# Attention and mixture of experts on one core: products with the values as one block per step, maxima turned as one square

## What is computed

```python
xt = jnp.transpose(x, (0, 2, 1))
q = xt @ Wq.T                                  # heads of dk = 16
scores = scale * jnp.einsum('bhqd,bhkd->bhqk', qh, qh)
logits = (scores * cmask + (1.0 - cmask) * NEG) * rmask
attn = jax.nn.softmax(logits, axis=-1)
ctx = jnp.einsum('bhqk,bhkd->bhqd', attn, qh)
out = ctx @ Wo.T                               # then transposed back
```

## The kernel before

| | TensorE | ScalarE | VectorE |
|---|---|---|---|
| 0 | | copy_hidden | |
| 1 | apply_probs, second half | copy_products | find_top |
| 2 | turn_max, project_q | copy_q | copy_max |
| 3 | turn_products | write_max | normalize |
| 4 | turn_values | | find_best, mark_best |
| 5 | turn_context | exp_gap, copy_v | |
| 6 | apply_probs, first half | copy_context | |
| 7 | project_out | | make_gate |

## Time and profile before

### The profile page before, as it was taken

How to read it: one execution, slowest core, us unless ns; L and a number is a source line. 1 busy time by engine, 2 the same in 40 slices (tenths; PEclk the granted TensorE clock), 3 DMA queues, 4 the chain that set the end, 5 groups by cost and what they waited for, 6 DMA issues and landing times.

```text
span 252.9 us, 5416 instructions
## 1 busy us (share of the span) xinstructions
PE 226.8 (90%) x1713; PEld 145.7 (58%) x1713; DVE 147.4 (58%) x403; ACT 132.9 (53%) x321; POOL 112.1 (44%) x206
## 2 busy tenths in 40 slices
PE   7988899989999999999999998499983799999970
PEld 5987556665666576657666554256541455555630
DVE  3786857868886888788878666436311122232320
ACT  2431577758767777777778887234311233333310
POOL 4755646624652464346001130631676146575351
PEclk9999999999999999999999999959999689999996
DMA  5685756997759766575533100460355024433100
GB/s 167 180 194 135 189 159 198 264 224 219 204 147 267 207 171 180 144 214 161 141 106 111 50 26 23 110 188 21 92 179 139 34 84 115 113 105 101 60 18 0
DMA packets 44731, 34.39 MB, mean 136 GB/s; under 512 B 5708, under 2 KB 42719, under 8 KB 44704
## 3 DMA queue, kind: packets, MB, share of 16 engines
q1 hardware_dynamic: 26896, 18.77, 27.3%
q0 software_dynamic: 2944, 8.24, 11.5%
q10 hardware_dynamic: 14864, 7.04, 11.1%
HBM read 16.91 MB, written 7.28 MB: 96 GB/s over the span
## 4 chain that ended last, share of the span: by engine, by line
PE 71%; DMA 8%; ACT 4%; DVE 3%; SPq 3%; issue 3%; ACTq 1%; another core or an unknown queue 1%; POOL 1%; POOLq 0%; DVEq 0%
PE bank L704 13%; PE bank L585 11%; PE bank L561 10%; PE bank L573 9%; PE bank L724 6%; PE bank L722 4%; PE bank L695 3%; DMA stack<-max_rows 3%; PE bank L614 3%; PE bank L526 3%; SPq L426 3%; ACT probs L785 3%; PE bank L606 2%; DMA stack<-parts 2%; PE bank L595 2%
## 5 line engine op out<-in xcount | busy, mean ns | idle before, releaser
L918 DVE TENSOR_REDUCE row_max<-bank 128x2 f32<-128x512 f32 x128 | 84.8, 687 | 24.1 <-PE bank L561 23.9
L785 ACT ACTIVATE probs<-bank 128x512 f32<-128x512 f32 x128 | 76.2, 600 | 25.2 <-PE bank L573 22.6
L561 PE MATMUL bank<-stack 96*128 96x256 bf16 x256 | 49.5, 274 | 1.7 <-DMA stack<-parts 1.5
L573 PE MATMUL bank<-stack 99*128 99x256 bf16 x256 | 49.0, 273 | 1.8 <-DMA stack<-max_rows 1.1
L386 POOL DMA_INDIRECT out<-y_sb,put_i x23 | 23.1, 1006 | 33.3 <-DVE y_sb L1184 28.0
L704 PE MATMUL bank<-gu_sb,gotT 128*128 x92 | 34.9, 506 | 0.0
L585 PE MATMUL bank<-probs,v_sb 128*32 128x256 f32 x512 | 34.3, 385 | 0.2 <-ACT probs L785 0.2
L561 PEld LDWEIGHTS bank<-stack 96*128 96x128 bf16 x256 | 21.2, 98 | 19.4 <-DVE row_max L918 10.4
L294 POOL TENSOR_TENSOR qm<-q_sb,cond_all 128x256 f32<-128x256 f32 x15 | 10.9, 729 | 45.4 <-ACT q_sb L770 45.4
L1176 DVE SCALAR_TENSOR_TENSOR act_sb<-silu,got,bank 128x176 f32<-128x176 f32 x23 | 9.1, 397 | 37.0 <-ACT silu L866 26.4
L376 POOL DMA_INDIRECT got<-rows_dram,take_i x23 | 22.5, 979 | 18.2 <-DVE take_i L1073 9.4
(11 more groups left out here) (154 smaller groups left out, 295.8 us busy)
## 6 DMA issues: line engine op xcount, KB each, us to landing
stack<-parts SPq DMA_DIRECT2D x96, 64.0 KB, 2.6
stack<-parts ACTq DMA_DIRECT2D x96, 64.0 KB, 2.7
gu_sb<-in_guT SPq DMA_DIRECT2D x8, 352.0 KB, 3.9
rows_dram<-h_sb SPq DMA_DIRECT2D x16, 132.5 KB, 2.4
x_sb<-in_x SPq DMA_DIRECT2D x16, 128.0 KB, 3.7
rows_dram<-in_x SPq DMA_DIRECT2D x4, 512.0 KB, 5.1
cond_all<-in_cond SPq DMA_DIRECT2D x12, 128.0 KB, 4.2
dn_sb<-in_dnT SPq DMA_DIRECT2D x4, 256.0 KB, 4.0
```

Source lines behind the costliest of these rows:

```text
L561: mm = t_.matmul(bank[h % 2][:, q * T:(q + 1) * T], stack[k][0:ROWS, 0, h, q * P:(q + 1) * P], stack[k][0:ROWS, 1, h, :], start=True, stop ...
L573: mm = t_.matmul(bank[2 + h % 2][:, q * T:(q + 1) * T], stack[k][0:ROWS2, 0, h, q * P:(q + 1) * P], stack[k][0:ROWS2, 1, h, :], start=True ...
L785: a.activation(probs[:, h, :, :].rearrange("p k t -> p (k t)"), bank[2 + h % 2][:, 0:NT * T], ACT.Exp, scale=float(DK) ** -0.5).then_inc(e ...
L918: v.tensor_reduce(row_max[:, b % 2, :, h:h + 1], bank[h % 2][:, 0:NT * T].rearrange("p (q k) -> p q k", q=NT), AX.X, ALU.max).then_inc(max ...
```

## The change

The products of a batch become one block of 32 matmuls in slot 2 of step s = b+3 (batch 15 keeps its old slots 6 and 1). `probs` gets a second home, and the exponentials wait for the products two batches back. The post work moves back: copy_products from slot 1 to 3, turn_products 3 to 4, normalize 3 to 4, turn_context 5 to 6, copy_context 6 to 7, project_out from slot 7 to slot 0 of the next step up to step 16, copy_hidden from 0 to 1, the router's choice to slot 2. turn_values goes from 4 to 5, copy_v from 5 to 6, project_q from 2 to 1. For the last batch most of the work stays where it was (`post`). The maxima are kept by head and half; both bfloat16 parts (2 x 16 columns) stand in one 128 x 128 tile whose other columns are zero, and TensorE turns that as one transpose. Then 32 rows of 128 values go to the stack, where there were 16 of 256.

```diff
+    NM = NH * NT
...
-        row_max = sb("row_max", [P, 2, NT, NH])
-        max_parts = sb("max_parts", [P, 2, NT, 2, NH], BF16)
-        max_rows = sb("max_rows", [2 * NH, 2, T], BF16)
-        probs = sb("probs", [P, NH, NT, T])
+        row_max = sb("row_max", [P, 2, NH, NT])
+        max_parts = sb("max_parts", [P, 2, P], BF16)
+        max_rows = sb("max_rows", [2 * NM, 2, P], BF16)
+        probs = sb("probs", [P, 2, NH, NT, T])
...
+        def post(s, slot):
+            return slot - 1 if s - 3 == B - 1 else slot
...
+            g.memset(max_parts[:, :, 2 * NM:P], 0.0).then_inc(consts_made, 1)
@@ split_max @@
-                g.tensor_copy(max_parts[:, k, :, 0, :], row_max[:, k, :, :]).then_inc(max_hi_made, 1)
+                maxima = row_max[:, k, :, :].rearrange("p h q -> p (h q)")
+                g.tensor_copy(max_parts[:, k, 0:NM], maxima).then_inc(max_hi_made, 1)
@@ turn_max @@
-                to = bank[VM][:, :].bitcast(BF16)
-                for q in range(NT):
-                    mm = t_.transpose(to[0:2 * NH, q * P:(q + 1) * P],
-                                      max_parts[:, b % 2, q, :, :].rearrange("p a h -> p (a h)"), ident_b[:, :])
-                mm.then_inc(max_turned, 1)
+                t_.transpose(bank[VM][:, :].bitcast(BF16)[:, 0:P], max_parts[:, b % 2, :], ident_b[:, :]).then_inc(max_turned, 1)
@@ TensorE, after both scores of slot h @@
-                    if h == 1 and there(s - 3):
+                    if h == 0 and there(s - 4) and s <= B:
+                        project_out(s - 4)
+                    if h == 1 and there(s + 3):
+                        project_q(s + 3)
+                    if h == 1 and s - 3 == B - 1:
                         apply_probs(s - 3, 1)
                     if h == 2:
                         if there(s - 1):
                             turn_max(s - 1)
-                        if there(s + 3):
-                            project_q(s + 3)
+                        if there(s - 3) and s - 3 < B - 1:
+                            apply_probs(s - 3, 0)
+                            apply_probs(s - 3, 1)
                         if s == B + 2:
                             table_early()
-                    if h == 3 and s == B:
+                    if h == post(s, 4) and there(s - 3):
+                        turn_products(s - 3)
+                    if h == 4 and s == B:
                         rank_early()
-                    if h == 3 and there(s - 3):
-                        turn_products(s - 3)
-                    if h == 4 and there(s):
+                    if h == 5 and there(s):
                         turn_values(s)
-                    if h == 6 and there(s - 2):
+                    if h == 6 and s - 2 == B - 1:
                         apply_probs(s - 2, 0)
-                    if h == 5 and there(s - 3):
+                    if h == post(s, 6) and there(s - 3):
                         turn_context(s - 3)
-                    if h == 7 and there(s - 3):
+                    if h == 7 and there(s - 3) and s >= B:
                         project_out(s - 3)
@@ exponential @@
-                if h % HG == 0 and b > 0:
-                    act.wait_ge(pv_done, NG * (b - 1) + h // HG + 1)
+                if h % HG == 0 and b > 1:
+                    act.wait_ge(pv_done, NG * (b - 2) + h // HG + 1)
@@ ScalarE, after the exponential and the DMA issue of slot h @@
-                    if h == 0 and there(s - 4):
+                    if h == (1 if s <= B else 0) and there(s - 4):
                         copy_hidden(s - 4)
-                    if h == 1 and there(s - 3):
-                        copy_products(s - 3)
                     if h == 2 and there(s + 3):
                         copy_q(s + 3)
+                    if h == (1 if s - 3 == B - 1 else 3) and there(s - 3):
+                        copy_products(s - 3)
                     if h == 3 and there(s - 1):
                         write_max(s - 1)
...
-                    if h == 5 and there(s):
+                    if h == 6 and there(s):
                         copy_v(s)
-                    if h == 6 and there(s - 3):
+                    if h == post(s, 7) and there(s - 3):
                         copy_context(s - 3)
@@ VectorE, after the reduction of slot h @@
-                    if h == 1 and there(s - 4):
+                    if h == (2 if s <= B else 1) and there(s - 4):
                         find_top(s - 4)
...
+                    if h == 2 and there(s - 4) and s < B:
+                        find_best(s - 4)
+                        mark_best(s - 4)
...
-                    if h == 3 and there(s - 3):
+                    if h == post(s, 5) - 1 and s - 3 == B - 1 or h == 4 and there(s - 3) and s - 3 < B - 1:
                         normalize(s - 3)
-                    if h == 4 and there(s - 4) and s < B:
-                        find_best(s - 4)
-                        mark_best(s - 4)
-                    if h == 4 and s == B:
+                    if h == 5 and s == B:
                         early_counts()
                         early_places()
```

More of the change, by code:

```diff
@@ L312, in split_max @@
                     pool.wait_ge(max_turned, b - 1)
-                g.tensor_copy(max_parts[:, k, :, 0, :], row_max[:, k, :, :]).then_inc(max_hi_made, 1)
+                maxima = row_max[:, k, :, :].rearrange("p h q -> p (h q)")
+                g.tensor_copy(max_parts[:, k, 0:NM], maxima).then_inc(max_hi_made, 1)
                 pool.wait_ge(max_hi_made, b + 1)
-                g.tensor_tensor(max_parts[:, k, :, 1, :], row_max[:, k, :, :], max_parts[:, k, :, 0, :],
+                g.tensor_tensor(max_parts[:, k, NM:2 * NM], maxima, max_parts[:, k, 0:NM],
                                 ALU.subtract).then_inc(max_lo_made, 1)
@@ L349, in _ @@
                     g.memset(ones_b[:, :], 1.0).then_inc(consts_made, 1)
-                    pool.wait_ge(consts_made, 5)
+                    pool.wait_ge(consts_made, 6)
                     g.affine_select(out=before[:, :], in_=before[:, :], compare_op=ALU.is_gt, fill=0.0, base=0,
@@ L546, in turn_max @@
                 if b == 0:
-                    pe.wait_ge(consts_made, 3)
-                to = bank[VM][:, :].bitcast(BF16)
-                for q in range(NT):
-                    mm = t_.transpose(to[0:2 * NH, q * P:(q + 1) * P],
-                                      max_parts[:, b % 2, q, :, :].rearrange("p a h -> p (a h)"), ident_b[:, :])
-                mm.then_inc(max_turned, 1)
+                    pe.wait_ge(consts_made, 4)
+                t_.transpose(bank[VM][:, :].bitcast(BF16)[:, 0:P], max_parts[:, b % 2, :], ident_b[:, :]).then_inc(max_turned, 1)
             def scores_for_max(b, h):
@@ L585, in apply_probs @@
                         mm = t_.matmul(bank[PV][c * VC:(c + 1) * VC, g * T:(g + 1) * T], v_sb[:, b % NV, k, HG * g + c, :],
-                                       probs[:, HG * g + c, k, :], start=(k == 0), stop=(k == NT - 1))
+                                       probs[:, b % 2, HG * g + c, k, :], start=(k == 0), stop=(k == NT - 1))
                 mm.then_inc(pv_done, 1)
@@ L624, in rank_early @@
                 pe.wait_ge(added, NE)
-                pe.wait_ge(consts_made, 6)
+                pe.wait_ge(consts_made, 7)
                 pe.wait_ge(max_done, NH * B)
@@ L782, in exponential @@
                 act.wait_ge(s2_done, NH * b + h + 1)
-                if h % HG == 0 and b > 0:
-                    act.wait_ge(pv_done, NG * (b - 1) + h // HG + 1)
-                a.activation(probs[:, h, :, :].rearrange("p k t -> p (k t)"), bank[2 + h % 2][:, 0:NT * T], ACT.Exp,
+                if h % HG == 0 and b > 1:
+                    act.wait_ge(pv_done, NG * (b - 2) + h // HG + 1)
+                a.activation(probs[:, b % 2, h, :, :].rearrange("p k t -> p (k t)"), bank[2 + h % 2][:, 0:NT * T], ACT.Exp,
                              scale=float(DK) ** -0.5).then_inc(exp_done, 1)
@@ L812, in write_max @@
                 act.wait_ge(max_copied, b + 1)
-                act.dma_start(stack[b % NSTACK][ROW_MAX:ROW_MAX + 2, 1, :, :], max_rows[:, k, :]).then_inc(max_in[k], 16)
+                act.dma_start(stack[b % NSTACK][ROW_MAX:ROW_MAX + 2, 1, :, :].rearrange("a h (q t) -> a (h q) t", q=NT),
+                              max_rows[:, k, :]).then_inc(max_in[k], 16)
             act.dma_start(wq_sb[:, :], wqT).then_inc(wq_in, 16)
@@ L917, in reduce_max @@
                     dve.wait_ge(max_lo_made, b - 1)
-                v.tensor_reduce(row_max[:, b % 2, :, h:h + 1],
+                v.tensor_reduce(row_max[:, b % 2, h, :],
                                 bank[h % 2][:, 0:NT * T].rearrange("p (q k) -> p q k", q=NT), AX.X, ALU.max).then_inc(max_done, 1)
@@ L924, in copy_max @@
                     dve.wait_ge(max_in[b % 2], 16 * (b // 2))
-                v.tensor_copy(max_rows[:, b % 2, :], bank[VM][:, :].bitcast(BF16)[0:2 * NH, 0:T]).then_inc(max_copied, 1)
```

(1 more changed line is left out.)

## The result

The changed kernel takes 275.25 us (median of 4 runs, 271.98 to 281.33) against 255.92 (4 runs, 254.92 to 257.26): ratio 1.071, 95% interval 1.060 to 1.082. The forecast was 269.5 in a range of 259.5 to 277, slower with 0.88. The profiled execution took 274.69 us with a span of 272.7, and it is compared here with the 252.9 of before.

What follows compares the result with a forecast made beforehand. The prediction took TensorE to bound the attention stage, with no slack. Its terms summed to +14.0 us on the profiled 254.78, giving 268.8, taken as 269.5 because the median is 1.0 higher; range 259.5 to 277.

Steps and rivals of the forecast that it cites:

- TensorE as the bound of the step: Attention stage: every piece of the 8.39 us step is a TensorE piece, with no slack.
- The block: Products on TensorE: one block of 32 takes 1.96 us instead of 2.20 for two of 16, 0.24 saved.
- The saving at the maxima: Turned maxima and the projection behind them on TensorE: 0.34 us saved per step, bounds 0.10 to 0.34.
- The two waits: TensorE waits 1.00 us for the products' copy and 0.53 for the context's copy; step 9.40 instead of 8.39.
- before step 3: Start of attention: batch 0's two half blocks of products move behind slot 2 of step 3, -2.0 us.
- steps 3 to 13: Middle of attention: 85.58 us becomes 94.0 at 9.40 a step, +8.4 us.
- steps 13 to 16: Later attention steps, with less work in each: 23.21 us becomes 26.4, +3.2 us.
- step 16 to the last half block: End of attention, one scores pair a slot: two steps of 8.1, 11.85 us becomes 16.2, +4.4 us.
- expert stage: The stage after attention: untouched by the change, 0 us.
- The late maxima: Rival: 256-byte pieces make every landing of the maxima's DMA take 4.92 us, 0.96 more a step, 281 us; chance 0.08.
- Only the first wait binds: Rival: the projection's weights find the context's copy in time, so only the products' copy holds TensorE; 259 to 260; chance 0.10.
- faster: Rival: the waits don't bind and TensorE runs its own 7.58 us, VectorE 7.9 a step; 247.7 us; chance 0.08.

Runs made afterwards that it cites:

- run 3: Changed kernel with the square undone (two transposes of 16 columns, 16 rows of 512 bytes in the maxima's DMA): 272.37 us.
- run 11: Changed kernel with maxima's DMA, products' copy and context's copy sooner, and the maxima turned as before (two transposes): 248.2 us, ratio 0.970 to the kernel before.
- run 4: Kernel before with only the maxima turned as one square, nothing moved: 251.19 us, ratio 0.998 to the kernel before.
- run 1: Changed kernel with ScalarE copying the products at the end of slot 2 instead of behind the exponential of slot 3: 268.76 us.
- run 2: Changed kernel with ScalarE copying the context in slot 6, behind the values, instead of behind the exponential of slot 7: 262.16 us.
- run 6: Changed kernel with both copies sooner (products at the end of slot 2, context in slot 6), maxima's DMA still in slot 3: 259.96 us.
- run 7: Changed kernel with maxima's DMA, then products' copy, at the end of slot 2, and context's copy in slot 6 ahead of the values: 246.68 us, ratio 0.966 to before.
- run 5: Changed kernel with the maxima's DMA issued at the end of slot 2, both copies left in place: 276.26 us.
- run 8: Kernel before with the square, and the maxima's DMA issued at the end of slot 2 instead of slot 3: 249.22 us, ratio 0.976.
- run 10: Kernel before with the square and the maxima's DMA in slot 2, once more: 250.3 us, ratio 0.978 to the kernel before.
- run 9: Changed kernel with maxima's DMA, products' copy and context's copy sooner, once more: 249.5 us, ratio 0.976 to the kernel before.

## Why the prediction was right, and what it mis-sized

**What bounds, and what the change saves.** TensorE as the bound of the step was right; with the waits removed the step follows TensorE's pieces again. The block was right to the hundredth (1.96: measured 1.86 and 0.10). The saving at the maxima was right as a sum and given to the wrong edit: turn and projection went from 0.84 to 0.06 + 0.43, 0.35 less (forecast 0.34), but the square has only some 0.02 to 0.06 of that, as whole steps with and without it differ (runs 3 and 11). By the rows the rest comes of moving `project_q` to slot 1, out from behind the turn (0.63 became 0.43), and of the turn standing right ahead of the block: two turns cost 0.15 there and 0.21 in the old order. No run moves `project_q` alone. The square is worth its 0.29 only in the old order (run 4).

**The two waits.** Right in place and nearly in size; the second shows in eight of ten steps, since in two the maxima's landing came later still. From the start of slot 2 (103.30 in the timeline of TensorE): products copied from 3.77 (forecast 3.69), L598 at 4.40 (4.33), L617 at 8.04 (7.96), next slot 2 at 9.46 (9.40). One detail was wrong: the exponential of slot 7 is held not by its scores but by the copy of the values ahead of it on ScalarE (109.56, 110.14, 110.42 in the chain above), which comes to the same time. Runs 1, 2, 6 and 7 show both waits: take away the one or the other and the step is 8.9, take away both and it is 8.6, take away the landing as well and it is 7.90.

**The sum, term by term** (from the chains before and after):

| term | forecast | measured |
|---|---|---|
| before step 3 | -2.0 | 33.91 - 35.88 = -2.0 |
| steps 3 to 13 | +8.4 | 98.02 - 85.58 = +12.4 |
| steps 13 to 16 | +3.2 | 26.53 - 23.21 = +3.3 |
| step 16 to the last half block | +4.4 | 18.64 - 11.85 = +6.8 |
| expert stage | 0 | 95.6 - 96.4 = -0.8 |
| sum | +14.0 | 272.7 - 252.9 = +19.8 |

(Slot 2 starts with its first scores in the chain: 33.91, 131.93 and 158.46, the last being the second half of a group of four; the blocks of 32 stand at 34.63, 132.42 and 158.73.) Two terms carry the 5.8 that was missing, with 4.0 and 2.4. In steps 3 to 13 four steps are 9.78, 11.54, 10.21 and 9.96 from block to block, 3.65 us above the 9.46 of the others. The longest of them in the timeline of TensorE:

```profile
81.20 0.39 PE L576 MATMUL bank<-stack 99*128 99x256 bf16 x2 [1.58 <-DMA stack<-max_rows]
...
82.32 1.01 PE L533 MATMUL bank<-x_sb,wq_sb 128*128 128x256 f32 x2
83.13 0.63 PE L564 MATMUL bank<-stack 96*128 96x256 bf16 x2
...
84.22 2.67 PE L588 MATMUL bank<-probs,v_sb 128*32 128x256 f32 x32
86.83 0.39 PE L564 MATMUL bank<-stack 96*128 96x256 bf16 x2
```

A wait for the maxima of 1.58, and then, in the chain, L533 at 0.85 instead of 0.43 and a block of 2.60 instead of 1.86: the granted clock is 0.50 from 82.5 to 85.5 us, the lower of the two levels (1.2 instead of 2.4 GHz), and was 1.00 throughout this stage before. Set against a step of 9.46, the landings account for 1.7 of the 3.65 us (1.2 in the step of 11.54, 0.5 in that of 9.96), the lower clock for 1.6 (in the steps of 11.54 and 10.21), and the 0.3 of the step of 9.78 goes through a DMA issue of ScalarE. So only two of the four have a landing in them, not three as I had put it ahead of run 5. The prediction had the smaller margin of the maxima (3.5 us), called it hidden up to 0.5, and put nothing into the sum for it. It had no term for the clock at all. Near the end it is the same: the step that begins at 167.47 has a block of 3.34 and lasts 9.63; in run 5 that step is at full clock and lasts 8.00, what the prediction worked out as 8.1. So 1.6 of the missing 2.4 there is clock. Of the other 0.8, some 0.5 is a wait that the working passed over: from slot 2 of step 16 to that of step 17 it is 8.62, and the scores at 167.08 had waited 0.47 for an exponential of ScalarE. The rest I haven't traced.

That 275.3 lies inside the range of 259.5 to 277 is thus in part luck. The range had room for some tenths a step for late DMAs, but the 3.2 us of lower clock had no term and no bound.

**The late maxima.** Nothing points to the 256-byte pieces as their cause. The same DMA in pieces of 512 bytes made TensorE wait six times in run 3, with landings of 3.9 to 4.8 us in its chain against 3.8 to 5.3 in the changed kernel. By the Trainium skill (DMA: Bandwidth & Descriptors, Specifications) transfers under 512 bytes are read, modified and written; no run here shows a cost of it. What counts is when the DMA is issued: from slot 2 there is no wait for it in the new order (runs 5 and 7), and one of 0.2 us in the old (run 8). The rival that every landing is late (0.08, 281) is refuted too: in the kernel after two steps of ten were longer for it.

**The chances.** "Only the first wait binds" and "faster" got 0.18 together and both were refuted by the list of waits. "Faster", that nothing holds TensorE, needed three instructions of ScalarE in other slots; then its number (7.9 us a step, 247.7 us) is what was measured (7.90, 246.7 and 249.5).

## What to carry to other kernels

When a step is moved back by a slot on every engine, its consumer may come to stand closer behind its producer than the latency between them: place the step again, engine by engine, with the measured start-to-start times, and ask of each copy what it is queued behind. A copy that depends only on the long block belongs right behind the block, where its engine is idle anyway (ScalarE for 1.41 us here), not behind the next head's work. And two savings at the same change from wide to narrow columns don't add up (0.29 in the old order, 0.02 to 0.06 beside the block).

## What the hardware showed that I had not expected

- The clock of TensorE fell to half (0.50 granted, for 3 to 7 us) inside the attention stage in six of the twelve profiled executions of other kernels than the one before, and never in that of before. The falls stood in or behind waits of TensorE of 1.49 us (run 4), 1.58 (after), 1.61 (run 10), 1.76 (run 9), 2.04 (run 5) and 2.26 (run 11). Waits of 1.57 (run 6), 1.48 (twice in run 1) and 1.42 (run 2) had no fall behind them, and the second fall of the kernel after, at 167.5, stood behind waits of at most 0.95, which run 5 has in the same steps without a fall. So the longest wait alone doesn't decide it, and what does isn't settled by these runs. Three of these waits, from the timelines of TensorE. Run 4, then run 5, the matmuls behind the wait already at the lower clock:

```profile
84.99 0.61 PE L572 MATMUL bank<-stack 99*128 99x256 bf16 x2 [1.49 <-DMA stack<-max_rows]
```

```profile
32.79 0.61 PE L564 MATMUL bank<-stack 96*128 96x256 bf16 x2 [2.04 <-DMA stack<-parts]
```

Run 6, at full clock:

```profile
112.84 0.39 PE L576 MATMUL bank<-stack 99*128 99x256 bf16 x2 [1.57 <-DMA stack<-max_rows]
```

- The maxima's DMA of 8 KB took 3.5 to 5.8 us to land where it stands in the chains, that is where something waited for it: 3.5 to 4.9 us in pieces of 512 bytes, 3.5 to 5.8 us in pieces of 256.
- Turning a 128 x 128 tile costs 0.06 us. Two turns of 16 columns cost 0.15 right ahead of the block on 32 columns; ahead of the projection, which is full width, they cost 0.21 and the projection behind them 0.63 instead of the 0.49 behind the square.
